# In steps with a bias: the maxima and scores of both halves first, then every product that adds a bias, then the values

## What is computed

```python
x = _layernorm(x + _L0_attn_ref(x, ...))              # A0: rotary, softmax(q k / sqrt(8)) v
x = _layernorm(x + _L0_xattn_ref(x, ctx, ctx))        # X0: + alibi bias, -inf above the diagonal
x = _layernorm(x + _L0_ffn_ref(x, ...))               # F0: attention among the 64 selected tokens of a sequence, causal
x = _layernorm(x + _L1_attn_ref(x, ...))              # A1: + Gaussian bias of rank 3
x = _layernorm(x + _L1_xattn_ref(ctx, ctx, x, mask))  # X1: energy = where(mask == 0, -1e20, energy)
x = _layernorm(x + _L1_ffn_ref(x, ...))               # 8 experts, top 2
```

## Time and profile before

| | |
|---|---|
| time, median of 3 runs | 1049.91 us (1047.21 to 1054.43) |
| the profiled execution | 1047.97 us, its span 1046.1 us |
| TensorE busy | 825.3 us (79%), 7108 products |
| VectorE busy | 636.2 us (61%) |
| ScalarE busy | 515.7 us (49%) |
| GpSimd busy | 182.8 us (17%) |
| L599, `add_bias`: X0, F0, X1 | 256 + 128 + 128 products |
| mean granted TensorE clock | 0.832 |

### The profile page before, as it was taken

How to read it: one execution, slowest core, us unless ns; L and a number is a source line. 1 busy time by engine, 2 the same in 40 slices (tenths; PEclk the granted TensorE clock), 3 DMA queues, 4 the chain that set the end, 5 groups by cost and what they waited for, 6 DMA issues and landing times.

```text
span 1046.1 us, 20646 instructions
## 1 busy us (share of the span) xinstructions
PE 825.3 (79%) x7108; PEld 426.3 (41%) x7109; DVE 636.2 (61%) x2000; ACT 515.7 (49%) x867; POOL 182.8 (17%) x313
## 2 busy tenths in 40 slices
PE   2787898889996639965659999479999935999960
PEld 1222333343443414434413334313333435999960
DVE  1577977676655814235458994377877344555567
ACT  1147876555565212313617877416666523666630
POOL 2232211111110201000401210210000023501414
PEclk8579989998998765557858999759999956999995
DMA  5466542322110122000622210142110051211212
GB/s 121 99 192 172 156 125 55 112 63 59 52 78 2 53 59 59 2 0 9 173 61 69 75 31 2 53 120 60 48 48 3 12 243 43 83 51 56 78 41 71
DMA packets 76074, 75.57 MB, mean 72 GB/s; under 512 B 21376, under 2 KB 65152, under 8 KB 75216
## 3 DMA queue, kind: packets, MB, share of 16 engines
q1 hardware_dynamic: 73504, 67.18, 22.8%
q0 software_dynamic: 2480, 7.21, 2.1%
HBM read 50.66 MB, written 23.13 MB: 71 GB/s over the span
## 4 chain that ended last, share of the span: by engine, by line
PE 64%; DVE 15%; issue 5%; ACT 4%; DMA 4%; POOL 4%; SPq 3%; POOLq 0%; DVEq 0%; ACTq 0%
PE PS L582 14%; PE PS L642 13%; PE PS L599 10%; PE PS L1796 7%; DVE MS L742 4%; PE PS L1806 4%; PE PS L656 3%; PE PS L589 3%; PE PS L326 2%; SPq L837 2%; POOL experts_x L1707 1%; PE PS L1001 1%; ACT X L1036 1%; PE PS L625 1%; PE PS L173 1%
## 5 line engine op out<-in xcount | busy, mean ns | idle before, releaser
L700 ACT ACTIVATE BIG<-PS 128x1024 f32<-128x1024 f32 (+2 forms) x288 | 260.8, 905 | 174.3 <-PE PS L599 123.6
L742 DVE TENSOR_REDUCE MS<-PS 128x2 f32<-128x512 f32 (+2 forms) x448 | 258.7, 593 | 130.1 <-PE PS L599 74.4
L582 PE MATMUL PS<-BIG 62*128 62x256 bf16 (+1 forms) x1088 | 226.9, 290 | 85.4 <-DVE MS L742 24.2
L589 PE MATMUL PS<-BIG 64*128 64x256 bf16 (+1 forms) x1088 | 216.2, 277 | 0.0
L642 PE MATMUL PS<-BIG,VA 128*32 128x256 f32 (+1 forms) x2176 | 171.6, 389 | 2.4 <-ACT OT L693 2.4
L582 PEld LDWEIGHTS PS<-BIG 62*128 62x128 bf16 x1088 | 65.5, 96 | 262.2 <-issue 143.5
L1796 PE MATMUL PS<-OT,VA 128*128 128x128 f32 x736 | 96.4, 278 | 0.4 <-ACT OT L1853 0.4
L1796 PEld LDWEIGHTS PS<-OT,VA 128*128 128x128 f32 x736 | 91.2, 195 | 0.6 <-ACT OT L1853 0.6
L806 POOL CAST MB<-MS 128x16 bf16<-128x16 f32 (+1 forms) x72 | 15.9, 221 | 410.5 <-DVE MS L742 192.3
L589 PEld LDWEIGHTS PS<-BIG 64*128 64x128 bf16 x1088 | 63.9, 95 | 20.3 <-issue 17.7
L693 ACT COPY OT<-PS 128x256 f32<-128x256 f32 (+1 forms) x144 | 51.7, 359 | 40.1 <-PE PS L642 39.6
(11 more groups left out here) (223 smaller groups left out, 1134.0 us busy)
## 6 DMA issues: line engine op xcount, KB each, us to landing
rows_q<-parts SPq DMA_DIRECT2D x32, 192.0 KB, 2.1
rows_k<-parts SPq DMA_DIRECT2D x32, 192.0 KB, 2.1
BIG<-rows_q SPq DMA_DIRECT2D x64, 96.0 KB
BIG<-rows_k SPq DMA_DIRECT2D x64, 96.0 KB
BIG<-in_ex_w SPq DMA_DIRECT2D x3, 2048.0 KB, 11.9
BIG<-rows_q SPq DMA_DIRECT2D x64, 64.0 KB
BIG<-rows_k SPq DMA_DIRECT2D x64, 64.0 KB
OT<-experts_x SPq DMA_DIRECT2D x46, 64.0 KB, 1.9
```

Of the source, the lines that this page charges most:

```text
L582: return nc.tensor.matmul(bank[:, first:first + kw], g.Q6[b.buf][rows, u, qt * P:(qt + 1) * P], g.K6[b.buf][rows, u, 0:kw], start=start, s ...
L589: return nc.tensor.matmul(g.bank[2 * (v % 2) + a][:, core.offset[kt]:core.offset[kt] + n], g.K6[b.buf][rows, v, kt * P:(kt + 1) * P], g.Q6 ...
L700: nc.scalar.activation(g.PT[v // 2 % 2][:, 2 * (v % 2):2 * (v % 2) + 2, 0:w], g.bank2[v % 2][:, :, 0:w], ACT.Exp, scale=SCALE).then_inc(se ...
L742: nc.vector.tensor_reduce(g.MS[:, 0:n, a, u], self.ring_bank["mx", step, a][:, 0:n * w] .rearrange("p (n k) -> p n k", n=n), axis=AX_X, op ...
```

## The change

The biases move out of `phase` into a new function `biases`, called after the second phase; it takes those of the maxima of both halves first, then those of the scores. If either item of the step has a bias, `values` moves behind it. The semaphores are raised by the same last products as before. Steps in which no item has a bias are as they were. In X1 the maxima have no product for the bias, so `mx_ready` is raised within the phase.

```diff
             for i in range(2):
                 if bm and i < bm.core.nqt:
                     mx = maxima(bm, bank, u, a, bm.core.nqt - 1 - i, not bm.core.matrix_bias(a) or i == 0)
                 if be and i < be.core.nqt:
                     st = scores(be, v, 1 - a, i, be.core.bias is None or i == 0)
-            if bm and bm.core.matrix_bias(a):
-                mx = add_bias(bm, bank, False)
+            if bm and not bm.core.matrix_bias(a):
+                mx.then_inc(self.mx_ready.sem, 1)
+            if be and a == 1 and be.core.bias is None:
+                st.then_inc(self.st_ready.sem, 1)
+
+        def biases(step, bm, be):
+
+            for a in range(2):
+                if bm and bm.core.matrix_bias(a):
+                    add_bias(bm, self.ring_bank["mx", step, a], False).then_inc(self.mx_ready.sem, 1)
             if be and be.core.bias is not None:
-                st = add_bias(be, g.bank[2 * (v % 2) + 1 - a], True)
-            if bm:
-                mx.then_inc(self.mx_ready.sem, 1)
-            if be and a == 1:
-                st.then_inc(self.st_ready.sem, 1)
+                bank = 2 * ((step - self.LAG) % 2)
+                add_bias(be, g.bank[bank + 1], True)
+                add_bias(be, g.bank[bank], True).then_inc(self.st_ready.sem, 1)
...
             phase(step, bm, be, 0)
             grp, kt = divmod(step - self.LAG - 3, 2)
-            values(grp, kt)
+            together = any(b and b.core.bias is not None for b in (bm, be))
+            if not together:
+                values(grp, kt)
             phase(step, bm, be, 1)
+            biases(step, bm, be)
+            if together:
+                values(grp, kt)
```

## The result

The changed kernel takes 1022.09 us (median of 4 runs, 1018.13 to 1024.63), the kernel before beside it 1049.01 us (4 runs). The ratio is 0.973, with a 95% interval of 0.968 to 0.978: it is faster by 2.7%, 26.9 us. The forecast was 1027 us. The profiled execution took 1018.13 us, its span 1016.3 us. The sum is right within 5 us, but its terms are not all right: X0 gives less than forecast, F0 more than twice as much.

A forecast was written before the change was run, and what follows sets the result against it. TensorE's row of instructions was taken to bound the three attention stages with a bias; gains of 8.5 (X0), 3.5 (F0) and 9.3 (X1), 21.3 us off 1047.97, gave 1027 us. Range 1012 to 1043 (forecast's own 1018 to 1036).

The forecast's parts named there:

- Two changes of split fewer per step: TensorE's row changes split three times instead of five; saves 0.15 us a step in X0, 0.19 X1, 0.22 F0.
- The read loop in X0: X0: second half's product waits for VectorE's two maxima reads of the step before; holds six of eight steps at 1.66 us.
- no loop: Rival, all three stages: every saved change of split counts and no wait for reads binds; 32.5 us gained, 1015; chance 0.10.
- longer loop: Rival: 0.15 us wait behind reads, read pair 1.16; X0's loop 1.90, net gain about 2, 1046 us; chance 0.18.
- The transposes: TensorE's row in X0 and X1: transposes in six of eight steps, put at 0.21 us each, about 1.3 per eight.
- X0's sum: Causal attention stage: 6.8 us from steps with maxima plus 1.7 from ten with scores alone, 8.5 us gained.
- X1's sum: Masked attention stage: 7.4 us from 54 steps with maxima plus 1.9 from ten with scores alone, 9.3 us gained.
- The waits behind a context: X1, twice in eight steps: VectorE's context delays the read; 0.05 us more where transposes follow, 0.25 where they don't.
- Steps with scores alone: Ten steps without maxima in each stage: save 0.17 us each in X0, 1.9 us in all in X1.
- F0: 7.9 for 3.5 us: Selected-token attention stage: first ten steps lose 2.0 us, the other 22 gain 3.3, ten with scores alone 2.2; 3.5 gained.
- the assumption that F0 stays at 1.2 GHz: F0: TensorE's row was priced at 1.2 GHz, 0.87 us instead of 1.10 a step, 0.22 less.
- No lower clock in X0: Rival denied: TensorE's pauses in X0 drop its clock to 1.2 GHz, up to 86 us more, 1113; chance 0.05.

The follow-up runs named there:

- short_reads: Changed kernel, but each VectorE read of maxima in X0 takes 256 of its 384 columns, computing less than the reference; 1014.88 us, ratio to before 0.970.
- f0_tail_before: Changed kernel, but F0's last ten steps (scores, no maxima) keep the old order; ratio to before 0.977.
- only_x0: Kernel before with the new order in X0 only; 1080.33 us against 1085.15, ratio 0.995.
- only_f0: Kernel before with the new order in F0 only; 1076.48 us against 1085.15, ratio 0.992.
- values_middle: Changed kernel, but the values stay between the two phases and only the biases are gathered at the step's end; 1047.92 us, ratio to before 1.002.

## Why the prediction was right, point by point

- **Two changes of split fewer per step: right.** X1's step is 1.66 us (forecast 1.67). In X0 the 128-column pair followed by a pair costs 0.06, not the 0.09 that I took between its bounds: in short_reads the pairs stand 0.18 apart (263.81 and 263.98, before rounding 0.178), 0.12 + 0.06. With biases 0.11 apart instead of 0.12, X0's row without transposes is 1.33 or 1.55 instead of 1.40 or 1.62 (263.81 to 265.73 in short_reads is 1.92, 0.37 of it transposes).
- **The read loop in X0: right, 1.67 us for 1.66.** A read that ends and a second half's product 0.06 later, 1.02 for two reads, 0.32 ahead of them: each term stands in the rows. Short_reads took the loop away and gained 0.8 per eight steps. The rivals "no loop" and "longer loop" (0.15 instead of 0.05 behind a read) fall with it.
- **The transposes: the term that was mis-sized.** I took 0.21 for each, as before, in six steps of eight. But the change moves them behind the values and so into another neighbourhood. Transposes of the context cost 0.37 (747.80 to 748.17), those of the maxima 0.10. That is four times 0.37 and two times 0.10: 1.7 per eight steps instead of 1.3. In X1 this 0.4 makes up the 0.3 by which eight steps miss the forecast (15.37 for 15.1); the row itself is 0.01 to 0.02 a step shorter than put. In X0 it changes which steps the loop binds: 2 x 1.70 and 2 x 1.92 with transposes of the context, 4 x 1.67 held by the loop, together 13.92 for the 14.00 measured. The rule of the Trainium skill on which the forecast drew ("TensorEngine Tiling (Array Packing)", Key Properties), that a change of mode drains TensorE, agrees with this 0.37 against 0.22 behind products of the same split; I counted the changes among products, biases and values and forgot to count those at the transposes.
- **X0's sum: 5.8 for 8.5 us.** Up to the last step with maxima it gains 3.6 where 6.8 stood, for the reason above (0.53 per eight instead of 0.9, so 4.0 by 60/8) and since its first ten steps, beside A0's last scores, lose 0.4 (19.6 to 20.0) where the sum had them gain. The ten steps of scores alone gain 2.3 (forecast 1.7).
- **X1's sum: 10.0 for 9.3 us.** The steps with maxima gain 7.0 (forecast 7.4), and the tail, from 24.1 to 21.0 us, 3.0 where 1.9 stood. The waits behind a context are as forecast, and in the steps with maxima no product waits for ScalarE: the copy follows the values' start by 0.71 as I had put it, and the values of the next step that needs the exponential wait for nothing.
- **Steps with scores alone: too small a term in X0 and X1.** I gave them the saving of the full steps, 0.17 and 0.19. But where a step has no maxima, the old order has a half's score products alone, and in the new one the scores of both halves, which use different halves of the array's rows, come together. In X1, before and changed:

```profile
827.28 0.39 PE L589 MATMUL PS<-BIG 64*128 64x256 bf16 x2
```

```profile
801.79 0.40 PE L589 MATMUL PS<-BIG 64*128 64x256 bf16 x4
```

Four products take the time of two. A step of scores without transposes falls from 1.85 to 1.44 us in X1, 0.41 instead of 0.19, and in X0, in one of the 128-wide ones, from 1.32 to 0.96. The dearer transposes take a part of it back.
- **F0: 7.9 for 3.5 us.** Its first ten steps behave as forecast (1.09 us each; 11.0 us with their ends). They took 9.9 before, not the 8.9 that I put, so they lose 1.1 instead of 2.0. The next sixteen steps, still at 1.2 GHz, take 20.9 instead of 23.3 us: 2.4, in line with the 3.3 put for 22 steps. Then the granted clock rises to 2.4 GHz. What follows until the last scores takes 14.0 us instead of 20.5 us, a gain of 6.5 where about 3 was forecast. The step that failed is the assumption that F0 stays at 1.2 GHz; f0_tail_before gives 2.6 us of the tail to the clock.
- **No lower clock in X0: right.** The slices wholly inside X0's products read 9 and the window 1.00, though TensorE pauses. The rule of the Trainium skill that I weighed as a rival ("TensorE: Matmul & The Clock Gate", A second HAM failure mode: psum-queue depth-cycling) did not act at pauses like these.
- **The sum was near since the errors cancel:** 2.7 too much in X0, 0.7 too little in X1 and 4.4 too little in F0. That the total came within 5 us is luck, the mechanism in X0 and X1 is not.

## What to carry to other kernels

Price a group of instructions by its neighbours, and count every change of split that a move makes or saves, the moved group's followers included: here the transposes that follow the values were not edited, and yet those of the context cost 0.16 us more each time. When work is gathered so that results become ready later and together, close the loop through every buffer they release, and let work that needs none of them stand behind them; the same gathering without that cover lost 12.6 us in X0 and with it all that the other stages gained. Look also at what becomes neighbours in steps that have only one kind of work: scores on different halves of the rows, brought together, took the time of one half's. Put groups with the same split side by side: values ahead of the first phase, biases and transposes together, is 0.7% faster still than the change.

## What the runs showed of the hardware

- The granted clock depended on the order of the same instructions. In the sixteen steps of F0 behind the first ten, TensorE starts 193 products in each kernel. With the order of before it was busy for all of the 23.30 us and stayed at 0.50 (only_x0). With the new order it was busy for 20.00 of 20.83 us and was then granted 1.00 (only_f0). With the biases gathered and the values left in the middle it was busy for 21.21 of 22.98 us and stayed at 0.50 (values_middle). A full busy row did not raise the clock; of two rows with pauses one was followed by a rise. When the first ten steps were shortened, the clock fell earlier in the stage (one trace). What decides it is not settled by these runs.
- Score products on different halves of the array's rows took the time of one pair when nothing stood between them (four in 0.40 us, two in 0.39, X1).
- The same transposes cost 0.37 us or 0.22 by what stands ahead of them, and the smaller transposes of the maxima 0.10 behind the values, where the forecast had 0.21 from the kernel before.
- From a read's end to the product that waits for it passed 0.05 to 0.06 us at a step's second half, and 0.15 at its first product (values_middle), which has other waits beside that one.
